# One 128x1536 GpSimd subtraction in place of three 128x512 ones for each weight chunk of the third layer's feed-forward

## The chip, the core and the metric

The kernel runs on one core of a Trainium2 chip. The metric is the device time of one execution in microseconds. Three runs of the kernel before gave 1284.37, 1284.82 and 1287.96 us (median 1284.82). The engines are called as the profile calls them: PE (TensorE matmul), PEld (its weight load), DVE (VectorE), ACT (ScalarE), POOL (GpSimd), SP (SyncE, which issues the DMAs).

## The reference, cut to what matters

Four layers run one after the other, each an attention and a feed-forward part, over 1024 rows of 512. The feed-forward of layer 2 (the third) is the one that the change touches. Its weights w1, w3 (1792x512) and w2 (512x1792) come as values with one scale for each block of 128x128:

```
def linear_dsv3(x, wq, w_scale):
    xq, xs = act_quant(x)                  # x / scale per 128 columns, then multiplied back
    xdq = (xq.reshape(T, K // BS, BS) * xs[:, :, None]).reshape(T, K)
    wdq = (wq.reshape(N // BS, BS, K // BS, BS) * w_scale[:, None, :, None]).reshape(N, K)
    return xdq @ wdq.T
```

The layer forms silu(x w1) * (x w3) and multiplies it by w2.

## The kernel before, in words

All matrix products of this part are done in a split form. A float32 operand is written as a high part (rounded to the format that PE reads fast, fp32r) and a low part (the rest), and a product is three matmuls: high by high, low by high, high by low. So each weight must be scaled, rounded and subtracted from itself before PE can use it.

The feed-forward of layer 2 goes through 28 chunks: 14 chunks of 128 hidden units, for each of two halves of 512 rows (`C = 2 * HC2`). A chunk `e` brings one 128x1536 block of weights: four 128x128 pieces each of w1 and w3, and one 128x512 piece of w2. It goes through one of four buffers (`W2BUFS = 4`), in these steps:

- SP (`load_chunk`) waits until PE has finished chunk e-4, and loads 768 KB into `W2_whole`.
- DVE (`scale_weights`, L1577) multiplies it by the block scales, in place.
- ACT (`weights_high`, L1116) copies it rounded to `W2_hi`.
- POOL (`weights_low`, L1940 to L1950) subtracts: `W2_lo = W2_whole - W2_hi`. `W2_lo` lies on the same bytes as `W2_whole`. Only the last instruction raises the semaphore `w_low`.
- PE waits for `w_low` once per chunk, at the start of `half_chunk` (L642), runs 12 matmuls for the gate and 12 for the up product (L662), and later 12 in `down` (L692).

Between these PE steps the hidden values are formed: ACT `gate_silu` (L1129) empties the gate's bank of PSUM, DVE `hidden` multiplies (L1593), ACT rounds (L1141), and DVE subtracts to get the low part `h_lo` (L1598). `down(2, e)` waits for `h_lo`. Gate and up have one bank each, so the gate of chunk e+1 can't start before the silu of chunk e.

The order on each engine is written out by hand. The first three chunks are done in slots among the last attention groups of layer 1 (`WEIGHTS2_SLOTS`, `PART2_SLOTS`, `HIDDEN2_SLOTS`), the others in a loop (`ffn2` on each engine) that also holds other work: on DVE `turn_context` (L1832), `residual` (L1840, L1845), `scale_rows` (L1478), `transposed_low` (L1467), rotations of queries and keys (`rope`), row maxima of the next attention (`row_max`, L1795); on POOL `scale_context` (L1994), `inverse_deviation` (L1937) and `stack_low` (L2011, L2015).

In the trace the weight tiles are called `W_lo_whole`, `W_hi` and `W_lo`. W_lo's three instructions of one chunk have equal shape, and the timeline merges them into one row with x3.

Of the kernel before, what the change touches and what calls it, by code (L numbers as in the profile page):

```python
# [22 lines left out]
F32 = mybir.dt.float32  # L23
# [4 lines left out]
ALU = mybir.AluOpType  # L28
# [5 lines left out]
KC = D // P  # L34
# [27 lines left out]
W2BUFS = 4  # L62
# [161 lines left out]
def program(nc, a, out):  # L224
    ctx = ExitStack()
    with ctx:
# [23 lines left out]
        def place_both(name, shape, at=None):  # L250

            whole = place(f"{name}_whole", shape, F32, at)
            return whole, nc.alloc_sbuf_tensor_at(name, shape, F32R, offset=names[f"{name}_whole"][0])
# [32 lines left out]
        for r, start in ((0, R + 36864), (1, WP)):  # L286
            at = [start]
            whole, lo = place_both(f"Wo{r}_lo", [P, KC, D], at)
# [6 lines left out]
        for l, start in ((0, WA), (2, WB), (3, WA)):  # L295
            Wqkv_hi[l], Wqkv_whole[l], Wqkv_lo[l] = [], [], []
            at = [start]
            for hh in range(2):
                Wqkv_hi[l].append(place(f"Wqkv{l}_hi{hh}", [P, KC, 384], F32R, at))
                whole, lo = place_both(f"Wqkv{l}_lo{hh}", [P, KC, 384], at)  # L300
# [60 lines left out]
        for r, where in enumerate((first, second)):  # L361
            at = [R + where["ring"]]
            whole, lo = place_both(f"ctxT{r}_lo", [P, RING, SEQ], at)
# [77 lines left out]
        W2_hi, W2_whole, W2_lo = [], [], []  # L441
        for i, start in enumerate((WA + 12288, WP, R, R + 12288)):
            at = [start]
            W2_hi.append(place(f"W2_hi{i}", [P, 3 * KC, P], F32R, at))
            whole, lo = place_both(f"W2_lo{i}", [P, 3 * KC, P], at)
# [37 lines left out]
        def part3(W, i):  # L483
            name, chunks = splits3[i]
            return W[name][:, :, chunks, :] if name == "V1" else W[name][:]
# [18 lines left out]
        def mark(name, per_layer):  # L504
            return Mark(nc, ctx, name, per_layer)
# [21 lines left out]
        w_low = mark("weights_low", [0, 0, 2 * HC2, len(splits3)])  # L527
# [1404 lines left out]
        def _(pool):  # L1932
            gp = nc.gpsimd
# [6 lines left out]
            def weights_low(l, i):  # L1940

                pool.wait_ge(*w_high.at(l, i + 1))
                if l == 2:
                    for k in range(0, 3 * KC, KC):
                        hi, whole, lo = (W[i % W2BUFS][:, k:k + KC, :] for W in (W2_hi, W2_whole, W2_lo))
                        ins = gp.tensor_tensor(lo, whole, hi.bitcast(F32), ALU.subtract)  # L1946
                else:
                    hi, whole, lo = (part3(W, i) for W in (W3_hi, W3_whole, W3_lo))
                    ins = gp.tensor_tensor(lo, whole, hi.bitcast(F32), ALU.subtract)
                ins.then_inc(w_low.sem, 1)  # L1950

            def hidden_low(e):

# [74 lines left out]
            def slot(r, G):  # L2028
# [16 lines left out]
                if r == 1 and (U, g) in SPLIT3_SLOTS:  # L2045
                    weights_low(3, SPLIT3_SLOTS[U, g])
# [6 lines left out]
                if r == 0 and (U, g) in WEIGHTS2_SLOTS:  # L2053
                    weights_low(2, WEIGHTS2_SLOTS[U, g])
# [5 lines left out]
            def ffn2():  # L2060

                C = 2 * HC2
                scale_context(0, RUN * GROUPS - 2)
                scale_context(0, RUN * GROUPS - 1)
                for e in range(3, C):
                    weights_low(2, e)
                    if e == 3:
                        inverse_deviation(2, SEQS - 1)
                    if e == 8:
                        pool.wait_ge(*x_done.at(1, TILES))  # L2070
                        set_pads(2)
                    if e == C - 7:
                        stack_low(2, 0, 0)
                    if e == C - 6:
                        stack_low(2, 0, 1)
                    if e == C - 2:
                        stack_low(2, 1, 0)
                stack_low(2, 1, 1)
# [261 lines left out]
```

## Time and profile before

| | |
|---|---|
| median of three runs | 1284.82 us (1284.37 to 1287.96) |
| the profiled execution's own time | 1287.96 us |
| its span | 1286.2 us |
| PE busy | 1153.2 us (90%), PEld 856.2 us (67%) |
| DVE busy | 832.1 us (65%) |
| ACT busy | 641.8 us (50%) |
| POOL busy | 490.9 us (38%), of which W_lo 117.1 us in 84 instructions |

The profiled execution is the slowest of the three: 1.8 us of its time lie outside the span, and it is 3.1 us above the median. The busy times are sums over the span and tell nothing yet of who waits for whom. Layer 2's feed-forward lies between about 550 and 860 us. The subtraction of the first chunk starts at 551.32 us, the one of the last at 832.21 us.

A row of the timeline reads: start, duration, engine, line, operation, output and inputs, shapes, count, and in brackets the idle time of the engine ahead of it with what ended it. The duration of a DVE or POOL instruction includes what it waits for inside the instruction, after its semaphores.

### The profile page before, as it was taken

How to read it: one execution, taken by the hardware profiler on the slowest of the kernel's cores; microseconds unless marked ns; L12 is line 12 of the kernel's file. 1: busy time of each engine (PE TensorE's matmuls, PEld its weight loads, DVE VectorE, ACT ScalarE, POOL GpSimd, SP SyncE). 2: the span in 40 equal slices, each digit the busy share in tenths (PEclk: the TensorE clock that was granted, in tenths of full speed). 3: DMA queues.
4: the chain of work that ended last, by engine and by line, in shares of the span. 5: the costliest groups of instructions: out<-in, count | busy, mean ns of one | idle time of the engine just before them, and what ended most of it. 6: DMA issues, size and time to landing. Idle time of an engine off the chain costs nothing.

```text
span 1286.2 us, 22381 instructions
## 1 busy us (share of the span) xinstructions
PE 1153.2 (90%) x8476; PEld 856.2 (67%) x8476; DVE 832.1 (65%) x1362; ACT 641.8 (50%) x1122; POOL 490.9 (38%) x692
## 2 busy tenths in 40 slices
PE   3999998989899899879999999998888888897997
PEld 3788877766656565546688887776666666675574
DVE  8743468886776755684644466538888778676543
ACT  3334357565555554553233433427755565566653
POOL 1000027454321111132555544506754565555642
PEclk7999989999999999989999999999999999999997
DMA  7000010030000100011242222201001000010000
GB/s 263 1 1 1 1 34 3 2 109 2 2 2 1 38 1 1 26 36 41 74 148 98 83 90 74 74 34 52 3 2 41 2 3 34 2 47 2 1 33 33
DMA packets 15260, 48.06 MB, mean 37 GB/s; under 512 B 2858, under 2 KB 6959, under 8 KB 14388
## 3 DMA queue, kind: packets, MB, share of 16 engines
q1 hardware_dynamic: 15156, 46.63, 10.4%
q8 instruction: 70, 1.15, 0.4%
q14 instruction: 34, 0.28, 0.1%
HBM read 44.00 MB, written 2.10 MB: 36 GB/s over the span
## 4 chain that ended last, share of the span: by engine, by line
PE 65%; DVE 15%; ACT 12%; issue 6%; DMA 1%; POOL 1%; POOLq 0%; ACTq 0%; DVEq 0%; SPq 0%
PE bank L662 19%; PE bank L778 14%; PE bank L692 9%; PE bank L906 8%; ACT probs L1364 6%; PE bank L881 4%; DVE negmax L1795 4%; PE bank L795 3%; PE bank L829 2%; ACT pv L1374 2%; PE bank L861 1%; PE bank L809 1%; DVE stats L1452 1%; DVE pvT L1821 1%; DVE W_lo_whole L1577 1%
## 5 line engine op out<-in xcount | busy, mean ns | idle before, releaser
L1795 DVE TENSOR_REDUCE negmax<-bank 128x4 f32<-128x1024 f32 (+1 forms) x256 | 250.1, 1016 | 78.8 <-PE bank L838 56.6
L1364 ACT ACTIVATE probs<-bank 128x1024 f32<-128x1024 f32 (+1 forms) x256 | 210.8, 862 | 27.2 <-PE bank L861 22.2
L2025 POOL TENSOR_SCALAR_AFFINE_SELECT probs<-probs 128x512 f32<-128x512 f32 x192 | 124.1, 665 | 116.5 <-ACT probs L1364 115.7
L1994 POOL TENSOR_TENSOR scaled<-pvT,recip 128x128 f32<-128x128 f32 x128 | 55.9, 437 | 286.2 <-DVE recip L1823 283.3
L1946 POOL TENSOR_TENSOR W_lo<-W_lo_whole,W_hi 128x512 fp32r<-128x512 f32 x84 | 117.1, 1423 | 99.3 <-ACT W_hi L1116 99.3
L829 PE MATMUL bank<-kT,qT 64*128 64x256 f32 (+1 forms) x1024 | 103.2, 295 | 24.4 <-DVE negmaxT L1813 8.4
L881 PE MATMUL bank<-probs,V 128*32 128x256 f32 (+1 forms) x2048 | 117.2, 346 | 4.0 <-DVE negmax L1795 2.7
L861 PE MATMUL bank<-qT,kT 64*128 64x256 f32 (+1 forms) x640 | 111.7, 378 | 4.7 <-DVE h_lo_whole L1623 1.8
L1374 ACT ACTIVATE pv<-bank 128x256 f32<-128x256 f32 x128 | 49.1, 383 | 132.5 <-PE bank L881 132.3
L829 PEld LDWEIGHTS bank<-kT,qT 64*128 64x128 f32 x1024 | 83.2, 187 | 44.3 <-issue 19.4
L1116 ACT ACTIVATE W_hi<-W_lo_whole 128x1536 fp32r<-128x1536 f32 x28 | 41.7, 1489 | 131.1 <-DVE W_lo_whole L1577 131.1
L662 PE MATMUL bank<-xT_hi,W_hi 128*128 128x512 f32 x224 | 91.2, 407 | 5.5 <-DVE xT_lo L1467 3.2
L778 PE MATMUL bank<-Wqkv,xT_whole 128*128 128x512 f32 (+1 forms) x256 | 87.7, 496 | 5.8 <-ACT probs L1364 5.8
L881 PEld LDWEIGHTS bank<-probs,V 128*32 128x32 f32 x2048 | 53.7, 109 | 57.5 <-issue 28.5
L662 PE MATMUL bank<-xT_hi,W_lo 128*128 128x512 f32 x224 | 88.5, 395 | 0.0
L662 PE MATMUL bank<-xT_lo,W_hi 128*128 128x512 f32 x224 | 88.4, 395 | 0.0
L778 PE MATMUL bank<-Wqkv_hi,xT_hi 128*128 128x384 f32 x192 | 68.9, 359 | 17.8 <-ACT probs L1364 17.7
L1141 ACT ACTIVATE h_hi<-h_lo_whole 128x512 fp32r<-128x512 f32 x72 | 45.5, 631 | 74.8 <-DVE h_lo_whole L1589 46.6
L861 PEld LDWEIGHTS bank<-qT,kT 64*128 64x128 f32 x640 | 57.5, 187 | 35.9 <-issue 30.0
L1316 ACT ACTIVATE qk<-bank 128x320 f32<-128x320 f32 (+1 forms) x64 | 30.5, 476 | 94.0 <-PE bank L778 85.8
L778 PEld LDWEIGHTS bank<-Wqkv,xT_whole 128*128 128x128 f32 x256 | 47.8, 192 | 42.3 <-issue 39.3
L795 PE MATMUL bank<-ident_r,qstack 128*128 128x128 f32 x512 | 55.8, 252 | 22.2 <-ACT probs L1364 21.6
(203 smaller groups left out, 2686.9 us busy)
## 6 DMA issues: line engine op xcount, KB each, us to landing
W_lo_whole<-in_w SPq DMA_DIRECT2D x28, 768.0 KB, 4.1
Wqkv_lo_whole<-in_Wqkv SPq DMA_DIRECT2D x6, 768.0 KB, 7.0
Wo_lo_whole<-in_Wo SPq DMA_DIRECT2D x4, 1024.0 KB, 5.0
Wqkv<-in_Wqkv SPq DMA_DIRECT2D x2, 1536.0 KB, 7.0
Wdown_whole<-in_Wd SPq DMA_DIRECT2D x1, 2816.0 KB, 14.6
x<-in_x SPq DMA_DIRECT2D x4, 512.0 KB, 5.2
out<-x SPq DMA_DIRECT2D x8, 256.0 KB, 2.0
V_lo_whole<-in_V SPq DMA_DIRECT2D x1, 1408.0 KB, 5.8
```

The source lines that it names most:

```text
L662: ins = mm(ps[:], lh, rh, start=(c == 0), stop=(c == len(terms) - 1))
L692: ins = mm(B.tensor(key), lh, rh, start=(j == 0 and c == 0), stop=(j == C - 1 and c == len(terms) - 1))
L778: ins = mm(ps[:, 0:width], lh, rh, start=(c == 0), stop=(c == len(terms) - 1))
L795: ins = nc.tensor.transpose(ps[:, p * P:(p + 1) * P].bitcast(F32R), A[l].qstack[tau][:, 8 * half + 2 * p:8 * half + 2 * p + 2, :] .rearran ...
L829: ins = mm(ps[:, par, pl * nk:(pl + 1) * nk], A[l].qT[u % 2][half, 2 * g + pl, qb * P:(qb + 1) * P], A[l].kT[u % 2][half, key_slot(l, g, p ...
L861: ins = mm(ps[:, par, pairs[0] * nq:pairs[1] * nq].rearrange("p (h q) -> p h q", h=n), A[l].kT[u % 2][r, key_slot(l, g, pairs[0]), kb * P: ...
L881: ins = mm(ps[32 * i:32 * i + 32, q0:SEQ], A[l].Vflat[u % 4][:, (kb * A[l].vh + kv) * CELL:(kb * A[l].vh + kv) * CELL + 32], A[l].probs[gi ...
L906: ins = mm(ps[:], lh, rh, start=(c == 0), stop=(c == len(terms) - 1))
L1364: nc.scalar.activation(A[l].probs[gi % 2][kb][:, :, q0 - kb * A[l].probs1:].rearrange("p (b h) q -> p b h q", b=2), B.tensor(key)[:, :, 0: ...
L1795: v.tensor_reduce(A[l].negmax[u % 2][:, qb, :].rearrange("p (b h) -> p b h", b=2)[:, :, 2 * g:2 * g + 2], B.tensor(key)[:, :, 0:2 * nk].re ...
L1946: ins = gp.tensor_tensor(lo, whole, hi.bitcast(F32), ALU.subtract)
L2025: gp.affine_select(out=blk, in_=blk, compare_op=ALU.is_ge, fill=0.0, base=0, pattern=[[0, 4], [1, P]], channel_multiplier=-1).then_inc(cau ...
```

## The change

The three instructions of a chunk become one over the whole 128x1536 block. The semaphore is raised once per chunk, as before. Nothing else changes; the 28 chunks have 84 instructions before and 28 after.

```
                 pool.wait_ge(*w_high.at(l, i + 1))
                 if l == 2:
-                    for k in range(0, 3 * KC, KC):
-                        hi, whole, lo = (W[i % W2BUFS][:, k:k + KC, :] for W in (W2_hi, W2_whole, W2_lo))
-                        ins = gp.tensor_tensor(lo, whole, hi.bitcast(F32), ALU.subtract)
+                    hi, whole, lo = (W[i % W2BUFS][:] for W in (W2_hi, W2_whole, W2_lo))
                 else:
                     hi, whole, lo = (part3(W, i) for W in (W3_hi, W3_whole, W3_lo))
-                    ins = gp.tensor_tensor(lo, whole, hi.bitcast(F32), ALU.subtract)
-                ins.then_inc(w_low.sem, 1)
+                gp.tensor_tensor(lo, whole, hi.bitcast(F32), ALU.subtract).then_inc(w_low.sem, 1)
```

On POOL, at the first chunk (in the slots of layer 1's attention), the program has before; `scaled` is the attention output of a group, `rstd` the inverse deviation of rows, and the numbers behind the names are buffers:

```order
L1994 TENSOR_TENSOR scaled_0_133<-pvT_0_127,recip_0_135 128x8x16
L1946 TENSOR_TENSOR W_lo_268<-W_lo_whole,W_hi_266 128x512 x3
L1994 TENSOR_TENSOR scaled_0_133<-pvT_1_128,recip_1_136 128x8x16
L1937 TENSOR_TENSOR rstd<-vareps,minus_half 128x2
L1994 TENSOR_TENSOR scaled_1_134<-pvT_0_127,recip_0_135 128x8x16
```

and now, at the same place on POOL:

```order
L1991 TENSOR_TENSOR scaled_0_133<-pvT_0_127,recip_0_135 128x8x16
L1947 TENSOR_TENSOR W_lo_268<-W_lo_whole,W_hi_266 128x1536
L1991 TENSOR_TENSOR scaled_0_133<-pvT_1_128,recip_1_136 128x8x16
L1937 TENSOR_TENSOR rstd<-vareps,minus_half 128x2
L1991 TENSOR_TENSOR scaled_1_134<-pvT_0_127,recip_0_135 128x8x16
```

Three instructions are one; what stands ahead and behind is the same.

On POOL, where the loop of `ffn2` begins (the fourth, fifth and sixth chunk), before:

```order
L1994 TENSOR_TENSOR scaled_1_134<-pvT_1_128,recip_1_136 128x8x16
L1946 TENSOR_TENSOR W_lo_277<-W_lo_whole,W_hi_275 128x512 x3
L1937 TENSOR_TENSOR rstd<-vareps,minus_half 128x2
L1946 TENSOR_TENSOR W_lo_268<-W_lo_whole,W_hi_266 128x512 x3
L1946 TENSOR_TENSOR W_lo_271<-W_lo_whole,W_hi_269 128x512 x3
```

and now:

```order
L1991 TENSOR_TENSOR scaled_1_134<-pvT_1_128,recip_1_136 128x8x16
L1947 TENSOR_TENSOR W_lo_277<-W_lo_whole,W_hi_275 128x1536
L1937 TENSOR_TENSOR rstd<-vareps,minus_half 128x2
L1947 TENSOR_TENSOR W_lo_268<-W_lo_whole,W_hi_266 128x1536
L1947 TENSOR_TENSOR W_lo_271<-W_lo_whole,W_hi_269 128x1536
```

The fifth and the sixth chunk stand next to each other: six instructions in a row before, two now. On PE, DVE and ACT the order is the same before and after.

## Rows read from the trace of the kernel before

**Rows 1.** The page's chain that ended last: shares of the span by engine.

```profile
PE 65%; DVE 15%; ACT 12%; issue 6%; DMA 1%; POOL 1%; POOLq 0%; ACTq 0%; DVEq 0%; SPq 0%
```

**Rows 2.** Waits, 570 to 870 us: who waited for whom, total, times, longest.

```profile
PEld bank L662 <- POOL W_lo L1946: 1.3, 2, 1.1
PE bank L662 <- POOL W_lo L1946: 0.9, 1, 0.9
```

**Rows 3.** Groups of POOL by form: busy us, mean ns | idle before.

```profile
L1946 POOL TENSOR_TENSOR W_lo<-W_lo_whole,W_hi 128x512 fp32r<-128x512 f32 x84 | 117.1, 1423 | 99.3 <-ACT W_hi L1116 99.3
...
L1949 POOL TENSOR_TENSOR U_lo<-U_lo_whole,U_hi 128x1408 fp32r<-128x1408 f32 x1 | 3.2, 3191 | 0.3 <-ACT U_hi L1092 0.3
```

**Rows 4.** Timeline: a 128x320 rotation alone, and beside a POOL instruction.

```profile
858.80 0.49 DVE L1787 TENSOR_TENSOR rope_cos<-rope_cos,rope_sin 128x320 f32<-128x320 f32 x1
...
907.26 1.90 POOL L1968 TENSOR_TENSOR Wqkv_lo<-Wqkv_lo_whole,Wqkv_hi 128x768 fp32r<-128x768 f32 x1
907.52 2.00 DVE L1787 TENSOR_TENSOR rope_cos<-rope_cos,rope_sin 128x320 f32<-128x320 f32 x1
```

**Rows 5.** Timeline: one chunk of the steady loop, and h_lo alone.

```profile
703.38 4.25 POOL L1946 TENSOR_TENSOR W_lo<-W_lo_whole,W_hi 128x512 fp32r<-128x512 f32 x3 [4.18 <-ACT W_hi L1116]
...
705.21 1.27 DVE L1598 TENSOR_TENSOR h_lo<-h_lo_whole,h_hi 128x512 fp32r<-128x512 f32 x1 [0.70 <-ACT h_hi L1141]
...
709.48 0.39 PE L692 MATMUL bank<-W_hi,h_hi 128*128 128x512 f32 x1
...
857.21 0.69 DVE L1598 TENSOR_TENSOR h_lo<-h_lo_whole,h_hi 128x512 fp32r<-128x512 f32 x1 [0.70 <-ACT h_hi L1141]
```

**Rows 6.** Timeline at the first chunk.

```profile
551.32 4.21 POOL L1946 TENSOR_TENSOR W_lo<-W_lo_whole,W_hi 128x512 fp32r<-128x512 f32 x3 [0.46 <-ACT W_hi L1116]
...
551.45 1.70 DVE L1845 TENSOR_TENSOR x<-x,gate 128x512 f32<-128x512 f32 x1
...
553.54 0.50 PE L829 MATMUL bank<-kT,qT 64*128 64x256 f32 x4 [0.96 <-DVE negmaxT L1813]
```

**Rows 7.** Timeline at the third chunk.

```profile
602.09 3.76 POOL L1946 TENSOR_TENSOR W_lo<-W_lo_whole,W_hi 128x512 fp32r<-128x512 f32 x3 [0.22 <-ACT W_hi L1116]
...
605.91 0.50 PE L662 MATMUL bank<-xT_hi,W_hi 128*128 128x512 f32 x1 [0.86 <-POOL W_lo L1946]
```

**Rows 8.** Timeline at the fourth chunk.

```profile
618.30 4.19 POOL L1946 TENSOR_TENSOR W_lo<-W_lo_whole,W_hi 128x512 fp32r<-128x512 f32 x3 [1.34 <-ACT W_hi L1116]
...
618.78 1.37 DVE L1598 TENSOR_TENSOR h_lo<-h_lo_whole,h_hi 128x512 fp32r<-128x512 f32 x1 [1.47 <-ACT h_hi L1141]
...
620.65 0.67 PE L906 MATMUL bank<-Wo_lo_whole,ctxT_lo_whole 128*128 128x512 f32 x1 [0.45 <-DVE ctxT_lo_whole L1832]
```

**Rows 9.** Timeline at the fifth and sixth chunk, and xn alone.

```profile
601.07 0.55 DVE L1478 TENSOR_SCALAR xn<-x,moments,rstd 128x512 f32<-128x512 f32 x1
...
633.00 8.35 POOL L1946 TENSOR_TENSOR W_lo<-W_lo_whole,W_hi 128x512 fp32r<-128x512 f32 x6
...
637.25 2.94 DVE L1478 TENSOR_SCALAR xn<-x,moments,rstd 128x512 f32<-128x512 f32 x2
...
644.49 0.57 ACT L1129 ACTIVATE silu<-bank 128x512 f32<-128x512 f32 x1
...
645.21 0.47 PE L662 MATMUL bank<-xT_hi,W_hi 128*128 128x512 f32 x1
```

**Rows 10.** Timeline at the chunk that starts at 821.97 us, and 11 us later.

```profile
821.97 4.22 POOL L1946 TENSOR_TENSOR W_lo<-W_lo_whole,W_hi 128x512 fp32r<-128x512 f32 x3 [4.09 <-ACT W_hi L1116]
...
823.80 1.27 DVE L1598 TENSOR_TENSOR h_lo<-h_lo_whole,h_hi 128x512 fp32r<-128x512 f32 x1 [0.70 <-ACT h_hi L1141]
...
826.26 0.44 PE L829 MATMUL bank<-kT,qT 64*128 64x128 f32 x4 [1.45 <-DVE negmax L1795]
...
837.19 0.50 PE L829 MATMUL bank<-kT,qT 64*128 64x256 f32 x4 [0.46 <-DVE negmax L1795]
```

**Rows 11.** Busy time by stretch: PE, PEld, DVE, ACT, POOL (counts), PE's clock, DMA.

```profile
577.00:582.00 5.00, 4.87 (x12) 3.84 (x13) 0.29 (x2) 1.11 (x2) 2.70 (x3) 0.50 0.46 159
```

## The prediction

> **What bounds the kernel now.** I read the chain of waits first. It runs through PE for 65% of the span, DVE 15%, ACT 12%, and through POOL for 1% [rows 1]. Then the waits in the stage that the change touches: PE and its weight loads wait for W_lo three times, 2.2 us together, though POOL works on it for 117.1 us in 84 instructions [rows 2, 3]. So a faster W_lo as such is worth little. What the reader should see next in the timeline is the DVE instruction that stands beside W_lo. The subtraction h_lo takes 0.69 us when POOL is idle and 1.27 us beside W_lo [rows 5]. It reads two tiles of SBUF, as W_lo does, and its wait is inside the instruction.
>
> **How long that wait is.** In the steady loop W_lo starts at 703.38, h_lo at 705.21. h_lo is free to run at 705.21 + 1.27 - 0.69 = 705.79, and the second of three 1.24 us pieces ends at about 703.38 + 2.5 = 705.9 [rows 5]. So DVE is let in when POOL goes from one instruction to the next, about 0.1 us ahead of the recorded end. At the first chunk the same: the addition x (two SBUF tiles of the same size, so 0.69 alone) starts 0.13 us behind W_lo and is free at 551.45 + 1.70 - 0.69 = 552.46, that is 1.14 us after W_lo's start, one piece less 0.1 [rows 6]. With a longer POOL instruction the wait is longer: a 128x320 rotation takes 0.49 us alone and 2.00 beside one of 128x768 that had started at 907.26. It became free at 907.52 + 1.51 = 909.03, 1.77 us after that start, and POOL's instruction ended at 909.16 [rows 4]. So what is held is held to the instruction's end, at least up to 768 columns.
>
> The Trainium skill's page "SBUF — State Buffer" (section "Who interferes with whom") speaks against this change: a VectorE instruction with two SBUF inputs and a GpSimd instruction that reads SBUF share a port, and whichever issues first has it "for the whole instruction". The trace agrees up to 1.77 us of holding [rows 4]. If the page holds at 1536 columns too, the sum below stands; without it, a hold that ends after 1.8 us whatever the length would make the three large terms about 0.6, 0.6 and 0, and the sum about +1 us.
>
> **The change part by part.**
>
> The instruction itself. 128x512 takes about 1.24 us uncontended (3.76 for three at the third chunk [rows 7]), 128x1408 takes 3.19 [rows 3]. That is (3.19 - 1.24) / 896 = 2.2 ns a column. So 128x1536 should take 3.19 + 128 x 2.2 ns = 3.47 us. The bounds are 3.19 from below and 4.25, three pieces with a DVE turn between them, from above [rows 5]. I take 3.47, by its nearest row. POOL then ends 0.3 us earlier where nobody contends, 0.8 us where h_lo used to cut in. Over 28 chunks that is 8 to 22 us of POOL time, and nearly all of it lies beside other work: POOL waits 99.3 us for W_hi anyhow [rows 3]. A DVE instruction that comes in behind W_lo is now free at start + 3.37 (3.47 less the 0.1).
>
> Steady chunks (about 20). h_lo becomes free at 703.38 + 3.37 = 706.75, ends at 707.44 instead of 706.48, 0.96 us later. PE needs it at 709.48 [rows 5], 2 us after. Cost 0. The next scaling waits for its DMA, which PE triggers.
>
> First chunk. x becomes free at 551.32 + 3.37 = 554.69 instead of 552.46: +2.2 us. Behind it on DVE wait the maxima in their turned form (negmaxT), for which PE waits at 553.54 with 0.96 us of idle time already [rows 6], then the next row maxima. The chain of waits goes through DVE there, and DVE has no idle time to absorb it. Cost +2.2.
>
> Second chunk. No DVE instruction with two SBUF inputs runs beside it. Cost 0.
>
> Third chunk. PE waits for it at 605.91, 0.86 us of idle, and nothing contends [rows 7]. POOL ends 3.76 - 3.47 = 0.3 us earlier. Gain -0.3.
>
> Fourth chunk. h_lo comes 0.48 us behind W_lo's start and is free at 618.78 + 1.37 - 0.69 = 619.46; now at 618.30 + 3.37 = 621.67: +2.2 us. Behind it on DVE is the turned context, and PE's output projection waits for that at 620.65, already 0.45 us idle [rows 8]. Cost +2.2.
>
> Fifth and sixth chunk, back to back from 633.00. Here two xn take 2.94 us where one alone takes 0.55 [rows 9]: each is let in between pieces. In the new order h_lo gets in at 633.00 + 3.37 = 636.37 and ends at 637.06, POOL's second instruction, which has been waiting, holds until 637.0 + 3.37 = 640.4, the two xn end at 641.5 instead of 637.25 + 2.94 = 640.2. The 1.3 us pass on: xT_lo, the next scaling, W_hi, then the silu at 644.49. Its end at 645.06 frees the gate's bank, 0.15 us before PE's next matmul at 645.21 [rows 9]. Cost 1.3 - 0.15 = +1.15.
>
> The chunk at 821.97. As in the steady loop h_lo ends 0.96 us later, but here a row maximum stands behind it, and PE waits for that at 826.26 (1.45 us idle). Eleven us later PE has 0.46 us of idle at 837.19 of the same kind [rows 10]; there W_lo's single instruction ends ahead of the delayed h_lo, so that idle time goes. Cost 0.96 - 0.46 = +0.5.
>
> The chunks with rotations behind h_lo: the same work takes its turns in another order and POOL's part is 0.3 us shorter. Cost between -0.3 and +0.3, taken as 0.
>
> Sum: 2.2 - 0.3 + 2.2 + 1.15 + 0.5 = +5.8 us (rounded). The bounds: with 3.19 for the instruction the three long waits shrink by 0.28 each and the third chunk gains that much more, sum +4.5; with 4.25 the four long waits grow by 0.78 each and the third chunk turns to +0.5, sum +9.5. Against the profiled execution's own 1287.96 us this makes 1293.8. That execution lies 3.1 us above the median, so from the median it is 1284.8 + 5.8 = 1290.6 us.
>
> **The rivals.**
>
> A. The port isn't held beyond what the rows show, or DVE gets in midway. Then the shorter instruction is what counts: -0.3 at the third chunk, and 0 to -0.3 for each wait that ended at a piece's end. For it: the longest hold in the rows is 1.77 us. Against: the 768-column row follows the instruction's end, no fixed time. Time: 1284.8 - 0.5 = 1284.3 (up to 1285.8 with a hold of 1.8 us). This is the side of not slower. It decides if h_lo in the steady loop stays under 1.3 us.
>
> B. x at the first chunk gets in ahead of POOL. The margin is 0.13 us [rows 6]. Then its wait disappears instead of growing: x ends 1.0 us earlier than now. POOL's first W_lo would only be pushed back by 0.7 us, where PE doesn't wait. The first term is -1.0 to 0 instead of +2.2. Against: what precedes is unchanged, and both start from the same DVE scaling. Time: 1290.6 - 2.2 - 0.5 = 1287.9.
>
> C. The longer gaps on PE cost clock. From 577 to 582 us, after a gap, PE was granted 0.50 of its speed (1.2 instead of 2.4 GHz), and 12 matmuls of 512 columns took 5 us [rows 11] instead of the 2.7 that 12 take in the steady loop. At 620.65 the gap grows from 0.45 to 2.65 us. If the clock falls there too, add 2.4: 1293.0.
>
> D. The delays are real but one of the two 2.2 us terms is made up again further on, by a wait that would have come anyway. For it: the chain names its releasers by inference. Against: in both places DVE goes on without idle time. With both halved: 1290.6 - 2.2 = 1288.4; with the third term gone as well 1287.2.
>
> **How the numbers follow.** Forecast (all terms, 1289 to 1292.5): 0.50. A: 0.11. B: 0.15. C: 0.10. D: 0.14. Three runs of the kernel before lie 3.6 us apart, so no change smaller than about 0.3% (3.9 us) can be told from none. The forecast is +0.45%. Slower by over 0.3%: forecast 0.48, C 0.10, and a third of B and D, 0.08: 0.66. Faster by over 0.3% needs A together with luck in the clock: 0.04. The rest, 0.30, is within. Range 1285.5 to 1294.0: the low end leaves out most of A, the high end is C with 1 us of scatter. The forecast's own range is 1289.0 to 1292.5.
>
> **What would show each step.** One W_lo lasts 3.4 to 3.5 us and POOL's busy time falls by some 20 us. The steady h_lo takes about 2.2 us instead of 1.27. At the first chunk x takes about 3.9 us instead of 1.70, at the fourth h_lo takes 3.6 instead of 1.37, and PE's idle times there grow to about 3.2 and 2.65 us. PE's wait at the third chunk shrinks from 0.86 to 0.6. The PE gap at 826 grows to 2.4, the one eleven us later goes. A steady PE loop stays without gaps. The prediction is wrong if h_lo keeps 1.27 us (A), if x is short (B), or if the waits are as said and the stage from 550 to 860 us isn't longer by 5 to 6 us (D).

## The result, and the profile of the changed kernel

The changed kernel took 1297.05 us (median of 13 runs, 1288.94 to 1303.39), the kernel before, run beside it on the same chip, 1288.05 us (13 runs, 1284.37 to 1292.33). The ratio is 1.0066 with a 95% interval of 1.0042 to 1.0090; by the medians the change costs 9.0 us. I had predicted 1290.6 us, which is +5.8 us on 1284.82, and a range of 1285.5 to 1294.0 us, which the measured time exceeds. Two parts make up the miss of 6.4 us. The median of before, taken from three runs, lay 3.2 us low; and the change cost 9.0 instead of 5.8 us. Measured twice more, in later comparisons, its ratio was 1.0091 (1.0067 to 1.0114) and 1.0082 (1.0049 to 1.0115). The 27 executions of the changed kernel in the three comparisons average 1298.4 us, and 135 of the kernel before, in the five comparisons that follow, 1288.1: +10.3 us. The first result lists 17 more executions of the changed kernel that its ratio doesn't use; with them 44 average 1297.9, or +9.8 us. So the effect is over one and a half times the forecast.

The page's chain by engine has hardly moved, and POOL has left it [rows 1]:

```profile
PE 65%; DVE 14%; ACT 12%; issue 6%; DMA 1%; POOL 0%; POOLq 0%; ACTq 0%; DVEq 0%; SPq 0%
```

In POOL's groups by form one instruction stands for three [rows 3]. 28 of them take 98.4 us, 3517 ns each with what they wait inside (I had said 3.47), and POOL's busy time fell from 490.9 to 475.2 us, by 15.7 (I had said some 20):

```profile
L1947 POOL TENSOR_TENSOR W_lo<-W_lo_whole,W_hi 128x1536 fp32r<-128x1536 f32 x28 | 98.4, 3517 | 117.2 <-ACT W_hi L1116 117.2
```

PE's waits for W_lo between 570 and 870 us shrank from 2.2 to 1.4 us [rows 2]:

```profile
PEld bank L662 <- POOL W_lo L1947: 0.8, 1, 0.8
PE bank L662 <- POOL W_lo L1947: 0.6, 1, 0.6
```

So all that the shorter instruction was good for is there. What stands beside it is the loss. The timeline of the changed kernel, in the order of rows 6, 7, 8, 9 and 10:

```profile
550.96 3.44 POOL L1947 TENSOR_TENSOR W_lo<-W_lo_whole,W_hi 128x1536 fp32r<-128x1536 f32 x1 [0.46 <-ACT W_hi L1116]
551.08 3.86 DVE L1845 TENSOR_TENSOR x<-x,gate 128x512 f32<-128x512 f32 x1
555.33 0.80 PE L829 MATMUL bank<-kT,qT 64*128 64x256 f32 x4 [3.12 <-DVE negmaxT L1813]
...
609.54 0.50 PE L662 MATMUL bank<-xT_hi,W_hi 128*128 128x512 f32 x1 [0.59 <-POOL W_lo L1947]
...
622.41 3.54 DVE L1598 TENSOR_TENSOR h_lo<-h_lo_whole,h_hi 128x512 fp32r<-128x512 f32 x1 [1.47 <-ACT h_hi L1141]
626.45 8.60 PE L906 MATMUL bank<-Wo_lo_whole,ctxT_lo_whole 128*128 128x512 f32 x16 [2.63 <-DVE ctxT_lo_whole L1832]
...
640.30 7.43 POOL L1947 TENSOR_TENSOR W_lo<-W_lo_whole,W_hi 128x1536 fp32r<-128x1536 f32 x2
644.28 4.19 DVE L1478 TENSOR_SCALAR xn<-x,moments,rstd 128x512 f32<-128x512 f32 x2
653.48 0.47 PE L662 MATMUL bank<-xT_hi,W_hi 128*128 128x512 f32 x1 [1.14 <-ACT silu L1129]
...
833.72 2.21 DVE L1598 TENSOR_TENSOR h_lo<-h_lo_whole,h_hi 128x512 fp32r<-128x512 f32 x1 [0.70 <-ACT h_hi L1141]
837.12 0.44 PE L829 MATMUL bank<-kT,qT 64*128 64x128 f32 x4 [2.31 <-DVE negmax L1795]
```

At the first chunk x takes 3.86 us instead of 1.70, and PE's idle time is 3.12 instead of 0.96. At the third chunk PE waits 0.59 instead of 0.86. At the fourth h_lo takes 3.54 instead of 1.37, and PE is idle for 2.63 instead of 0.45. At the fifth and sixth the gate's matmul waits 1.14 us for the silu. At the late chunk PE is idle for 2.31 instead of 1.45, and the idle time of 0.46 eleven us later is gone. Each of these waits is within 0.1 us of what the prediction said.

The 16 matmuls behind the fourth chunk's wait are something else: they take 8.60 us, and before they took 7.11:

```profile
620.65 7.11 PE L906 MATMUL bank<-Wo_lo_whole,ctxT_lo_whole 128*128 128x512 f32 x16 [0.45 <-DVE ctxT_lo_whole L1832]
```

And x is released late only once, but the work behind it runs slowly for long. Busy time by stretch (the columns of rows 11), first in the kernel before, then in the changed one:

```profile
555.00:580.00 25.00, 16.92 (x157) 11.44 (x150) 18.80 (x32) 13.50 (x19) 6.91 (x10) 0.85 0.19 64
580.00:600.00 20.00, 20.00 (x115) 11.75 (x115) 8.44 (x16) 5.54 (x8) 1.50 (x2) 0.94 0.01 2
600.00:640.00 40.00, 38.07 (x198) 26.23 (x195) 23.89 (x37) 16.63 (x21) 21.68 (x19) 1.00 0.24 80
836.00:866.00 30.00, 28.87 (x166) 23.17 (x164) 9.69 (x16) 8.32 (x15) 1.40 (x2) 1.00 0.10 36
```

```profile
555.00:580.00 25.00, 21.68 (x158) 13.59 (x158) 19.27 (x31) 11.03 (x15) 2.10 (x5) 0.53 0.10 33
580.00:600.00 20.00, 17.85 (x90) 10.65 (x91) 6.13 (x11) 7.11 (x12) 4.01 (x3) 0.91 0.13 41
600.00:640.00 40.00, 36.18 (x191) 23.52 (x190) 24.84 (x42) 14.73 (x19) 14.92 (x10) 0.96 0.18 60
836.00:866.00 30.00, 28.88 (x152) 22.26 (x153) 11.58 (x13) 5.82 (x10) 5.32 (x5) 0.94 0.17 60
```

PE's clock is the third number from the end. In the 25 us behind the 3.12 us gap PE was granted 0.53 of 2.4 GHz, that is 1.2 GHz nearly all the time, where it had 0.85. It runs 158 matmuls in 21.68 busy us instead of 157 in 16.92. Behind the gaps at 626 and 837 us the clock falls a little too (0.96 and 0.94, where it had 1.00). This is what the sum lacked.

### The profile page after: what moved, and what is told of

It is laid out like the page before. It is cut to its first block, busy times and chain, and to the rows that moved or that the text cites. A ratio compares the mean times of both kernels' runs of the same rounds, so it can differ in the third digit from the quotient of the medians.

```text
span 1303.8 us, 22325 instructions
## 1 busy us (share of the span) xinstructions
PE 1166.5 (89%) x8476; PEld 864.2 (66%) x8476; DVE 846.7 (65%) x1362; ACT 643.0 (49%) x1122; POOL 475.2 (36%) x636
## 3 DMA queue, kind: packets, MB, share of 16 engines
q8 instruction: 70, 1.15, 0.4%
## 4 chain that ended last, share of the span: by engine, by line
PE 65%; DVE 14%; ACT 12%; issue 6%; DMA 1%; POOL 0%; POOLq 0%; ACTq 0%; DVEq 0%; SPq 0%
PE bank L662 18%; PE bank L778 14%; PE bank L692 8%; PE bank L906 8%; ACT probs L1364 6%; PE bank L881 5%; DVE negmax L1795 3%; PE bank L795 3%; PE bank L829 2%; ACT pv L1374 2%; PE bank L861 1%; PE bank L809 1%; DMA W_lo_whole<-in_w 1%; DVE stats L1452 1%; DVE W_lo_whole L1577 1%
## 5 line engine op out<-in xcount | busy, mean ns | idle before, releaser
L1947 POOL TENSOR_TENSOR W_lo<-W_lo_whole,W_hi 128x1536 fp32r<-128x1536 f32 x28 | 98.4, 3517 | 117.2 <-ACT W_hi L1116 117.2
L829 PE MATMUL bank<-kT,qT 64*128 64x256 f32 (+1 forms) x1024 | 105.9, 302 | 25.1 <-DVE negmaxT L1813 10.3
L881 PE MATMUL bank<-probs,V 128*32 128x256 f32 (+1 forms) x2048 | 121.6, 356 | 3.1 <-DVE negmax L1795 1.7
L861 PE MATMUL bank<-qT,kT 64*128 64x256 f32 (+1 forms) x640 | 114.8, 388 | 6.0 <-DVE h_lo_whole L1623 3.1
L829 PEld LDWEIGHTS bank<-kT,qT 64*128 64x128 f32 x1024 | 86.4, 194 | 44.2 <-issue 18.5
L1116 ACT ACTIVATE W_hi<-W_lo_whole 128x1536 fp32r<-128x1536 f32 x28 | 41.7, 1488 | 136.4 <-DVE W_lo_whole L1577 136.4
L1598 DVE TENSOR_TENSOR h_lo<-h_lo_whole,h_hi 128x512 fp32r<-128x512 f32 x48 | 68.7, 1432 | 34.3 <-ACT h_hi L1141 34.3
L778 PEld LDWEIGHTS bank<-Wqkv,xT_whole 128*128 128x128 f32 x256 | 47.9, 192 | 42.5 <-issue 39.4
```

The costliest lines, as they stand in the source:

```text
L778: ins = mm(ps[:, 0:width], lh, rh, start=(c == 0), stop=(c == len(terms) - 1))
L829: ins = mm(ps[:, par, pl * nk:(pl + 1) * nk], A[l].qT[u % 2][half, 2 * g + pl, qb * P:(qb + 1) * P], A[l].kT[u % 2][half, key_slot(l, g, p ...
L861: ins = mm(ps[:, par, pairs[0] * nq:pairs[1] * nq].rearrange("p (h q) -> p h q", h=n), A[l].kT[u % 2][r, key_slot(l, g, pairs[0]), kb * P: ...
L881: ins = mm(ps[32 * i:32 * i + 32, q0:SEQ], A[l].Vflat[u % 4][:, (kb * A[l].vh + kv) * CELL:(kb * A[l].vh + kv) * CELL + 32], A[l].probs[gi ...
L1947: gp.tensor_tensor(lo, whole, hi.bitcast(F32), ALU.subtract).then_inc(w_low.sem, 1)
```

## The experiments

No kernel below leaves work out; the fills and pauses add work whose result nobody reads. Ratios are to the kernel before, on the same chip, with their 95% intervals.

To compare traces without the scatter of the rest I use one measure throughout: the start of DVE's scaling of a chunk (L1577), which happens 28 times in each trace. In the kernel before the scalings of the first and the second chunk start at

```profile
547.98 1.75 DVE L1577 TENSOR_TENSOR W_lo_whole<-W_lo_whole,block_scales 128x1536 f32<-128x1536 f32 x1
...
572.26 1.75 DVE L1577 TENSOR_TENSOR W_lo_whole<-W_lo_whole,block_scales 128x1536 f32<-128x1536 f32 x1
```

and in the changed kernel at

```profile
547.62 1.75 DVE L1577 TENSOR_TENSOR W_lo_whole<-W_lo_whole,block_scales 128x1536 f32<-128x1536 f32 x1
...
577.31 1.75 DVE L1577 TENSOR_TENSOR W_lo_whole<-W_lo_whole,block_scales 128x1536 f32<-128x1536 f32 x1
```

24.28 us against 29.69. The table under the third group of experiments has this measure for ten traces.

**First group: single chunks, and an order that avoids the waits.** The three-piece loop stays for some chunks (`i` is the chunk, counted from 0). These are the conditions in place of the one of the kernel before, one for each kernel:

```
-                if l == 2:                          # three pieces for all chunks
+                if l == 2 and i != 0:               # only the first chunk in one
+                if l == 2 and i != 3:               # only the fourth
+                if l == 2 and i in (0, 3, 4, 5, 26):  # these five in three, 23 in one
```

> Only the first chunk's subtraction is one 128x1536 instruction; the other 27 chunks have three of 128x512 as in the kernel before. Theory 1 (the port is held to the instruction's end): the addition x lasts 3.9 us as in the changed kernel, PE's gap behind it is about 3 us, all later holds are as before (fourth chunk's h_lo 1.4 us), and the time lies 2.2 us above the kernel before, plus what PE's clock takes (it was granted 0.65 and 0.56 in the 30 us behind that gap in the changed kernel, 0.93 in the kernel before), so +2 to +6 us. Rival (the clock is lost by chance or elsewhere, whatever the gap): +2.2 us, and the granted clock from 555 to 580 us stays at 0.9.

> Only the fourth chunk's subtraction is one instruction. Theory 1: x is 1.70 us as before, h_lo of the fourth chunk 3.5 us, PE's gap ahead of the output projection 2.6 us, time +2.2 us and up to 1.5 us more if PE's clock falls in the projection as it did in the changed kernel (16 matmuls in 8.60 us against 7.11). The clock from 555 to 580 us stays as in the kernel before. Rival (the term is made up again further on): time within 1 us of the kernel before.

> The first, fourth, fifth, sixth and twenty-seventh chunk have three pieces as before, the other 23 chunks one instruction. Theory 1: all of the loss lies in those five chunks, so the time is that of the kernel before within 2 us (-0.3 us from the third chunk), though h_lo lasts 2.2 us in the steady loop. Rival (the 23 longer waits in the steady loop cost time or clock too): at least a third of the changed kernel's loss stays, +3 us or more.

In the fourth kernel all chunks are in one, and POOL waits until DVE is through with what would be held:

```
+                if l == 2 and i == 0:
+                    pool.wait_ge(*x_done.at(1, 4))
+                if l == 2 and i in (3, 26, 27):
+                    pool.wait_ge(*h_low.at(2, {3: 3, 26: 25, 27: 26}[i]))
...
-                    if e == 3:                      # inverse_deviation on POOL
+                    if e == 4:
```

> All 28 chunks have one instruction, but POOL issues it behind the DVE instruction that it would block where PE waits for that one: at the first chunk behind x, at the fourth behind h_lo, at the twenty-seventh and twenty-eighth behind h_lo, and at the fifth POOL does the subtraction ahead of rstd. Theory 1 (order of issue decides): x and these h_lo last 0.69 us, PE's gap behind x nearly goes, the time is 2 to 3 us below the kernel before (x -1.0, third chunk -0.3, fourth -0.7, the two last -1.0), more if the low clock at 577 us goes too. Rival (a long instruction costs by its length, wherever it stands): slower than the kernel before.

Measured: first chunk alone 1293.37 us, ratio 1.0032 (1.0002 to 1.0061); its profiled execution took twice its time (last section) and shows nothing of the change. (The expectation sets 0.93 against the changed kernel's 0.65 and 0.56 of 550 to 565 and 565 to 580 us; the kernel before has 0.89 and 0.86 in these stretches.) Fourth alone 1293.83 us, 1.0043 (1.0019 to 1.0067). Five chunks kept in three pieces: 1289.15 us, 1.0007 (0.9982 to 1.0033), though the steady h_lo takes 2.2 us there as in the changed kernel. So 23 long instructions with their longer holds cost nothing that can be told from scatter (the interval ends at +4.3 us; the table below has them at -0.2): the loss lies in the five chunks that the prediction had named.

The fourth chunk alone has the same slow matmuls as the changed kernel, with a first chunk that is undisturbed (PE, L906):

```profile
620.60 8.50 PE L906 MATMUL bank<-Wo_lo_whole,ctxT_lo_whole 128*128 128x512 f32 x16 [2.63 <-DVE ctxT_lo_whole L1832]
```

The ordered kernel took 1286.01 us, 0.9985 (0.9956 to 1.0015). x and h_lo take 0.69 us at the first and the fourth chunk. But beside the moved instruction of the fifth chunk an x of the next rows now lasted 2.46 us, 1.77 of them waiting, and a gap of 0.77 us behind the silu was the price.

**Second group: is it the wait, the instruction, or the clock?** The changed kernel again:

> The changed kernel once more, beside the next three. Theory 2 (the waits cost 6 us, and the two long gaps on PE cost clock behind them, some 3 us): the ratio to the kernel before is 1.0066 as in the first comparison, within 0.003, and a second profile again shows PE's granted clock well under 0.9 between 555 and 580 us and the 16 matmuls of the projection in more than 7.11 us. Rival (the low clock of the first profile was one of the scattered episodes that both kernels have): 0.9 or more in this profile.

The changed kernel with unread matmuls on PE in its two early gaps, 12 ahead of the score matmuls at the first chunk and 10 ahead of the output projection:

```
+            def keep_busy(bank, n, chunk):
+                ...
+                for _ in range(n):
+                    mm(B.ps[:, bank, :], w[:, 0, :], w[:, 2 * KC:3 * KC, :].rearrange("p n o -> p (n o)"), start=True, stop=True)
...
+                    if r == 0 and (U, g) == (13, 3):
+                        keep_busy(QKV_BANK, 12, 0)
...
+                keep_busy(3, 10, 2)
                 project_out(1, SEQS - 1, 0, 3)
```

> The changed kernel, with matmuls that nobody reads in PE's two long gaps (12 of 512 columns, 2.7 us, ahead of the score matmul that waits for negmaxT; 10, 2.3 us, ahead of the output projection), written to banks that are free there. The waits themselves stay: x 3.9 us, h_lo 3.5 us. Theory 2: the clock stays up behind the gaps (over 0.9 between 555 and 580 us; the 16 projection matmuls in 7.1 us instead of 8.6), and the time falls by 2 to 4 us against the changed kernel though more work is done. Rival (the clock has nothing to do with the gaps): no gain, or 0 to 1 us lost by the fill.

The kernel before with its three pieces, and an unread DVE instruction of 2.4 us behind x at the first chunk and behind h_lo at the fourth:

```
+            def pause():
+                v.tensor_reduce(minus_half[:, TILES - 1:], ident[:].unsqueeze(1).to_broadcast([P, 17, P]), AX.XY, ALU.max)
```

> The kernel before with its three pieces, and in place of the longer holds a DVE reduction of about 2.3 us that nobody reads, once behind x at the first chunk and once behind h_lo at the fourth. No port is held for longer than before. Theory 2 (what counts is that DVE is late at these two places): the same gaps on PE (about 3.2 and 2.7 us) and nearly the changed kernel's loss, +5 to +8 us. Rival (something else in the long instruction costs the rest, as the 23 steady chunks): +4.5 us or less.

And the first chunk alone once more, for its trace:

> The kernel of the first experiment once more, since its profiled execution took 2655 us (everything on PE twice as long) and can't be read. Theory 2: x lasts 3.9 us, the gap behind it is 3.1 us, the clock between 555 and 580 us is under 0.9, the start of the second chunk's scaling is 5 us later than in the kernel before, and the ratio is 1.0032 within 0.003. Rival: a start 2.2 us later, with the clock at 0.9 or more.

Measured: changed 1299.54 us, 1.0091 (1.0067 to 1.0114). Filled 1296.07 us, 1.0071 (1.0047 to 1.0095), with six runs each, so by ratio the fill's gain of 0.2% is not shown. Pause 1296.78 us, 1.0060 (1.0036 to 1.0084). The kernel to set beside it is the one with the first and the fourth chunk in one (third group, 1.0052): late DVE work at these two places costs as much with short POOL instructions, so nothing else in the long instruction has to be looked for. First chunk alone 1292.13 us, 1.0028 (1.0004 to 1.0051).

What the traces show is sharper. In the filled kernel, with h_lo still held for 3.58 us:

```profile
549.06 3.01 PE L916 MATMUL bank<-W_hi 128*128 128x512 f32 x12 [0.94 <-ACT probs L1376]
...
617.81 2.43 PE L916 MATMUL bank<-W_hi 128*128 128x512 f32 x10
...
620.64 7.11 PE L906 MATMUL bank<-Wo_lo_whole,ctxT_lo_whole 128*128 128x512 f32 x16 [0.40 <-DVE ctxT_lo_whole L1844]
```

DVE is as late as in the changed kernel, the 16 matmuls behind it take 7.11 us again. In the kernel with pauses, where the gap is 2.78 us, they take 10.15:

```profile
627.17 10.15 PE L906 MATMUL bank<-Wo_lo_whole,ctxT_lo_whole 128*128 128x512 f32 x16 [2.78 <-DVE ctxT_lo_whole L1833]
```

And the clock of 555 to 580 us is 0.53 with pauses and 0.54 with only the first chunk in one; in the filled kernel it is 0.81:

```profile
555.00:580.00 25.00, 17.10 (x137) 12.10 (x138) 16.86 (x28) 12.63 (x18) 5.72 (x6) 0.81 0.20 64
```

**Third group: where the rest is.** By now the waits explained 5.8 us and the measurement was about 10. The changed kernel a third time, one with a third fill (8 matmuls, meant for the late gap), and the two early chunks alone:

> The changed kernel once more, beside the two below on one chip. Both theories: ratio to the kernel before 1.007 to 1.009. The profile should again show the granted clock at 0.5 to 0.7 from 555 to 580 us, 0.96 from 600 to 640 and 0.94 from 836 to 866, behind PE gaps of 3.1, 2.6 and 2.3 us.

> The changed kernel, with unread matmuls on PE in its three long gaps: 12 at the first chunk, 10 ahead of the output projection, 8 ahead of the row scores at about 835 us. DVE's waits stay (x 3.9, h_lo 3.5 and 2.2 us). Theory (PE's empty gaps cost clock, about 5 us in the three places together): granted clock at 1.00 from 600 to 640 and from 836 to 866, and the ratio to the changed kernel beside it -0.35 to -0.4%, so about 1.0045 of the kernel before, what the waits alone make. Rival (the clock falls elsewhere in most executions and the three places tell nothing of the mean): no difference to the changed kernel, within 0.15%.

> Only the first and the fourth chunk as one instruction, the 26 others in three. Theory (these two places carry waits of 4.4 us and 4 to 5 us of clock): ratio to the kernel before 1.006 to 1.007, at most 0.2% below the changed kernel. Rival (the clock adds nothing in the mean): 1.0035, the waits alone.

Then the late chunks alone (`i not in (4, 5, 26)` keep three pieces), and all but the two early ones (`i in (0, 3)` keep three):

> Only the fifth, the sixth and the twenty-seventh chunk as one instruction, the 25 others in three. Both theories: the PE gaps of 1.15 us at the fifth and sixth chunk and of 2.3 to 2.4 us at about 825 us come back. The waits alone (1.15 + 0.5 us) make the ratio 1.0013. Theory (this place carries clock too, or something the sum left out): 1.003, the 4 us by which the changed kernel lies above the one with the first and the fourth chunk alone. Rival (those 4 us are scatter between chips): 1.001 to 1.0015.

> The complement of e15: the first and the fourth chunk in three instructions, the 26 others in one. The waits alone make +1.35 us, ratio 1.001. Theory (the late places carry more than their waits): 1.003, as e16. If e16 stays at 1.001 and this is at 1.003, the loss is in the steady chunks; if both are at 1.001, the clock behind the two early gaps carries the whole excess of the changed kernel.

Measured: changed 1298.44 us, 1.0082 (1.0049 to 1.0115). Three fills 1297.30 us, 1.0064 (1.0037 to 1.0092). Its third fill missed: it stood at 845.81 us, 13 us behind the gap, and lengthened PE's full stretch by 1.98 us. The two early chunks alone 1295.34 us, 1.0052 (1.0023 to 1.0080). The three late ones 1290.89 us, 1.0018 (0.9987 to 1.0050). All but the two early ones 1290.35 us, 1.0024 (0.9991 to 1.0058). The late chunks alone cost about as much as all but the early ones (0.18% and 0.24%), which again leaves little for the steady ones. Early and late together, 0.52% and 0.24%, make 0.76%, the changed kernel's 0.82% within the intervals. The intervals of the last two reach below 1, so their size rests on the traces.

Ten traces (the kernel before; the changed one three times; those with single chunks) sorted by whether a chunk goes in one instruction or in three. The stretches go from scaling to scaling, the last one to the final h_lo. Each cell is a mean of the starts' differences, with the lowest and highest:

| stretch (chunks from 0) | in three | in one | more | waits as predicted |
|---|---|---|---|---|
| 0 to 2, by chunk 0 | 50.35 (48.5 to 51.4) | 54.09 (51.1 to 55.0) | +3.7 | +2.2 |
| 2 to 5, by chunk 3 (2 in three) | 32.02 (32.00 to 32.04) | 35.72 (35.56 to 35.87) | +3.7 | +2.2 |
| 2 to 5, by chunk 3 (2 in one) | 31.74 (31.72 to 31.76) | 35.47 (35.40 to 35.60) | +3.7 | +2.2 |
| 5 to 6, by chunks 4 and 5 | 10.59 (10.58 to 10.59) | 11.55 (11.55 to 11.56) | +1.0 | +1.15 |
| 6 to 27, by the chunks between | 189.0 (187.5 to 190.0) | 188.8 (187.9 to 189.3) | -0.2 | 0 |
| 27 to the end, by chunk 26 | 27.96 (27.5 to 28.4) | 29.59 (28.67 to 30.28) | +1.6 | +0.5 |

Chunk 2's own term is the difference of lines two and three: -0.3. The sum is 3.7 - 0.3 + 3.7 + 1.0 - 0.2 + 1.6 = +9.5 us, of the 10.3 that the executions differ by in the mean.

The same stretches in the two filled kernels: chunks 0 to 2 take 53.27 and 53.21 us. Chunks 2 to 5 take 33.94 in both, which is 31.74 plus the 2.2 us of the wait alone. So at the fourth chunk the 1.5 us beyond the wait are the clock behind the gap, and filling the gap gives them back in full: with the gap of 2.63 us the 16 matmuls take 8.50 to 8.80 us in all five traces, with the fourth chunk in three pieces or the gap filled 7.10 or 7.11 in all seven. At the first chunk four of five executions with the gap take 54.3 to 55.0 us and have a clock of 0.53 to 0.70 from 555 to 580; the fifth (first and fourth alone) has the same gap of 3.12 us, but its row is

```profile
555.00:580.00 25.00, 17.62 (x166) 11.42 (x167) 20.21 (x33) 14.14 (x19) 6.31 (x9) 0.91 0.18 56
```

and it takes 51.1 us. Nor does the short gap keep the clock up. Of the five executions with the first chunk in three pieces and a gap of 0.96 us, three have 0.93, 0.89 and 0.85, but two (the late chunks alone; all but the early ones) have 0.73 and take 51.3 us:

```profile
555.00:580.00 25.00, 18.44 (x135) 12.46 (x136) 15.64 (x24) 11.37 (x16) 5.76 (x8) 0.73 0.20 64
```

Executions of like clock differ by little more than the wait of 2.2 us: 51.1 against 48.5 us at 0.91 and 0.93, 54.3 against 51.3 at 0.70 and 0.73. The 1.5 us beyond the wait are a difference between two means of five executions that spread over 3 and 4 us. That the long gap makes the loss of clock deeper and more frequent here is likely (0.53 or 0.54 stands only behind long gaps), but its size isn't shown, and the fill doesn't settle it: the two filled kernels, at 0.81 and 0.86, still lie 2.9 us above the mean in three.

At the end too the gap makes the loss likely and not sure: with the gap of 2.3 to 2.5 us, three executions show a low stretch behind it and take 30.1 to 30.3 us, and two don't and take 28.67, which is the wait alone (+0.7). No execution with the short gap there (1.37 to 1.58 us) shows one.

By ratio the fills are weaker: 16 executions of the two filled kernels average 0.17% below the 14 of the changed one beside them (-0.35% to +0.02%, by resampling the executions), and one of the two carries the misplaced fill.

**Fourth group: pieces and order as remedies.** Six pieces of 128x256 (`for k in range(0, 3 * KC, KC // 2)`):

> Each chunk's subtraction is six instructions of 128x256 instead of three of 128x512. Theory (a DVE instruction with two SBUF inputs waits for the end of the POOL instruction that stands): the waits shrink with the piece, x to 1.2 us (from 1.70), the steady h_lo to between 0.7 and 1.3 us, h_lo of the fourth chunk to about 1.0 us. POOL needs 4.2 to 4.5 us a chunk, so PE's wait at the third chunk grows by 0.5 us. Time -0.5 us against the kernel before, within its scatter (-2 to +1). Rival (each POOL instruction costs DVE a wait of its own kind, whatever its length): x and h_lo as before or longer, and the time above the kernel before.

The kernel before with 12 unread matmuls ahead of the second chunk's first matmul, where it has a gap of 3.15 us itself:

> The kernel before with its three pieces, and 12 matmuls of 512 columns that nobody reads (2.7 us) in the gap of 3.1 us that PE has ahead of the first gate product, at 574 us. Theory 2 (a long gap costs clock right behind it): the 12 gate matmuls behind it start 0.23 us apart instead of 0.43, and the time falls by up to 2.4 us. Rival (the clock there was lost by the thin work of the 25 us before, not by the one gap): the fill itself runs slow, the gate matmuls stay at 0.43, and the time stays or grows by up to 3 us, since the fill at half speed is longer than the gap.

The ordered kernel mended (POOL's waits as above, `rstd` in its old place, chunks 4 and 5 in three pieces), and the same with that fill (cut where `...` stands):

```
+                if l == 2 and i == 0:
+                    pool.wait_ge(*x_done.at(1, 4))
+                if l == 2 and i in (3, 26, 27):
+                    pool.wait_ge(*h_low.at(2, {3: 3, 26: 25, 27: 26}[i]))
+                if l == 2 and i in (4, 5):          # three pieces, as before
...
```

> Mends a fault of the first ordered version, where the fifth chunk's subtraction, moved ahead of rstd, held up another x for 1.8 us and made a PE gap of 0.77 us at 643 us. Here rstd is back in its place, the fifth and sixth chunk have three pieces, all others one instruction, behind x or h_lo at the first, fourth, twenty-seventh and twenty-eighth chunk. Expected: no PE gap at 643, all else as in the first ordered version, so 0.8 us faster than that, and 2 to 3.5 us (0.2 to 0.3%) faster than the kernel before. Rival (length by itself costs): at or above the kernel before.

> The second ordered version with the 12 unread matmuls in the gap of 3.1 us ahead of the first gate product. If the fill keeps the clock (theory 2), 2 us faster than the second ordered version and 4 to 5 us faster than the kernel before; by the rival of the fill in the kernel before, no faster than the second ordered version, or up to 3 us slower.

Measured: six pieces 1288.73 us, 1.0000 (0.9977 to 1.0023). Its x takes 1.16 us and the fourth chunk's h_lo 0.82, but POOL pays more starts, 136.4 us against 117.1 [rows 3]:

```profile
L1946 POOL TENSOR_TENSOR W_lo<-W_lo_whole,W_hi 128x256 fp32r<-128x256 f32 x168 | 136.4, 846 | 86.8 <-ACT W_hi L1116 86.8
```

What it wins early (chunks 0 to 2 take 47.9 us) it loses in the steady chunks (6 to 27 take 191.1, longer than in any trace of the table). So finer pieces than three bring nothing that can be measured. The fill in the kernel before cost: 1291.96 us, 1.0023 (1.0000 to 1.0047); in the mended one 1291.57 us, 1.0023 (0.9998 to 1.0047). It missed its place. It waited for its bank, stood behind the gap instead of in it, and ran slowly itself. In the kernel before it took 5.42 us instead of the 2.7 that 12 take at the full clock, in the mended one 4.35:

```profile
575.49 5.42 PE L916 MATMUL bank<-W_hi 128*128 128x512 f32 x12 [3.28 <-ACT probs L1375]
```

Whether that older gap can be filled with profit stays open.

The mended ordered kernel took 1284.56 us, 0.9969 (0.9946 to 0.9993). That is 4 us below the kernel before; the changed kernel, which didn't run beside it, was above the kernel before in all its three comparisons. And 26 of the 28 chunks go in one instruction. Its timeline at the first and the fourth chunk:

```profile
549.35 0.69 DVE L1845 TENSOR_TENSOR x<-x,gate 128x512 f32<-128x512 f32 x1
550.19 3.46 POOL L1957 TENSOR_TENSOR W_lo<-W_lo_whole,W_hi 128x1536 fp32r<-128x1536 f32 x1 [1.42 <-DVE x L1845]
...
613.44 0.69 DVE L1598 TENSOR_TENSOR h_lo<-h_lo_whole,h_hi 128x512 fp32r<-128x512 f32 x1 [1.47 <-ACT h_hi L1141]
614.28 3.44 POOL L1957 TENSOR_TENSOR W_lo<-W_lo_whole,W_hi 128x1536 fp32r<-128x1536 f32 x1 [2.65 <-DVE h_lo L1598]
```

x and h_lo run first, in 0.69 us, and POOL's long instruction begins when they are through, 0.15 us later. Chunks 0 to 2 take 47.8 us here and chunks 2 to 5 31.1, both below every one of the ten traces above. With the last stretch, 27.04 us, that makes 4.5 us against the means in three, of which the first chunk's 2.6 may be in part chance.

## Why the prediction was right in its waits and wrong in its size

- **One W_lo lasts 3.4 to 3.5 us**: right, 3.44 to 3.50 uncontended. POOL's busy time fell by 15.7 us, not by some 20.
- **The port is held to the instruction's end, also at 1536 columns**: right. x was free at 551.08 + 3.86 - 0.69 = 554.25, 3.29 us after POOL's start and 0.15 us ahead of its recorded end. Rival A is out: the steady h_lo takes 2.21 us, not under 1.3. The page "SBUF — State Buffer" of the Trainium skill ("Who interferes with whom") writes "for the whole instruction" of VectorE's two-port modes; of an instruction with two SBUF inputs, as here, it says that it contends, and the prediction joined the two. The traces agree with that reading: 3.29 us of holding here, 1.77 in the rows before.
- **x behind POOL, not ahead (rival B)**: B is out; POOL still starts 0.12 to 0.13 us ahead in all three traces of the changed kernel.
- **Steady chunks at nothing**: right (-0.2 us over 21 stretches, each mean spread over 1.4 to 2.5 us; ratio 1.0007 with the five chunks in three pieces).
- **Third chunk -0.3, fifth and sixth +1.15**: right, -0.3 and +1.0.
- **Delays made up (rival D)**: out. The two 2.2 us terms are there in full: the fourth chunk's by 33.94 against 31.74 us, the first chunk's by 2.6 and 3.0 us between executions of like clock.
- **The late chunk +0.5**: the wait was near (+0.7 where the clock stayed), and 1.5 us of clock come on top in three of five executions.
- **The clock (rival C) is where it failed.** The prediction wrote "If the clock falls there too, add 2.4: 1293.0", for the gap at 620 us alone, and gave it 0.10. For the gap of 3.1 us at the first chunk, the longest that the change makes, and for the late one it put nothing, and gave no reason. The runs show +1.5 us at the fourth chunk in each of five executions, which the fills give back; +1.5 in the mean at the first chunk, with the doubt said above; and +0.9 in the mean at the late one beside a wait of 0.7. Together that is 3.9 us, on 5.6 us of waits. So the 2.4 of rival C was too much for its one place and stood for too few of them. The kernel before had shown what the first gate product meets behind a gap, half the clock [rows 11]:

```profile
577.13 0.77 PE L662 MATMUL bank<-xT_hi,W_hi 128*128 128x512 f32 x1 [3.15 <-DVE xT_lo L1467]
```

  The prediction read it as an oddity of one place, not as a price on each gap that the change lengthens.
- **The base.** "From the median" made 1284.82 of three runs the foot of the number. Over 135 more executions the kernel before averages 1288.1. This is 3.2 us of the miss of 6.4. The range allowed 1 us for scatter, though the text itself calls the three runs 3.6 us apart. From the profiled execution's own 1287.96 us the same sum gave 1293.8, as the prediction also says; that would have been nearer, by luck and not by a better mechanism.
- **The bounds of the sum.** By the prediction's own terms they come to +4.6 and +9.7, where it has +4.5 and +9.5. Its range, up to 1294.0, leaves out the upper one, which would have been 1294.5. The measured +9.0 to +10.3 lies near that bound, but not for its reason: one W_lo took 3.5 us, not 4.25.

What stays open: what decides whether the clock falls at the first chunk, where it fell in four of five executions behind the long gap and in two of five behind the short one; 0.8 us between the sum of the stretches and the difference of the means (0.3 us with all 44 executions), which is below what the runs can resolve; and whether the fills gain time by ratio, which was not shown.

## What to carry to other kernels

The length of a GpSimd instruction is worth looking at not for its own time but for the VectorE instruction with two SBUF inputs that gets in behind it: it waits to the end, so make the piece short where something urgent comes late, or let the urgent one issue first and keep the long piece. When a change lengthens an idle time of TensorE, put two prices on it, the gap and the clock behind it, look for a gap of that length in the rows of before to size the second, and read it from more than one execution: here it came in five of five at one place and not always at two others. Take the base time from more than three runs when the effect is below 1%.

## What the runs showed of the hardware that I had not expected

- One execution of the kernel with only the first chunk in one took 2655.63 us, where its eleven others took 1286.72 to 1295.56. PE was busy 99% of it, and its matmuls took twice their time: the high by high ones of the gate and up products 838 ns instead of 407. The granted clock that its profile shows is 1.00 all the same, so that number doesn't show this kind of slowness. DVE's, ACT's and POOL's busy times (807.2, 666.3 and 477.0 us) were within 4% of the kernel before. What caused it stays open. This row is from its groups by line:

```profile
L662 PE MATMUL bank<-xT_hi,W_hi 128*128 128x512 f32 x224 | 187.6, 838 | 0.4 <-DVE xT_lo L1467 0.4
```

- Times of POOL's subtraction by size, all uncontended: 128x256 0.72 us, 128x512 1.26, 128x1408 3.19, 128x1536 3.44 to 3.50. That is about 2.1 ns a column and 0.18 us to start.
- Executions of one and the same kernel lie up to 1.5% apart: in the first comparison of single chunks 35 of the kernel before took 1278.20 to 1297.02 us; 12 of the mended one took 1279.55 to 1291.82. In the traces the starts of chunks agree within 0.3 us where the clock does the same each time (the stretch from 2 to 5, sorted as in the table), and differ by 3 to 4 us where it may fall or not (0 to 2).
